# Edge convolution with features on partitions, its product turned on TensorE between the block sums

## What is computed

```python
h = x @ W_in                                                  # (N, 128)
W_ij = ssp(f_ij[:, 0, :] @ Wf1 + bf1) @ Wf2 + bf2             # (E, 128), f_ij has 32 values per edge
W_ij = W_ij * f_ij_cutoff                                     # one number per edge
x_ij = h[idx_j] * W_ij                                        # idx_j = dst: h of the sorted ends
out  = jax.ops.segment_sum(x_ij, idx_i, num_segments=N)       # idx_i = src: unsorted ends
y    = ssp(out @ Wo1 + bo1) @ Wo2 + bo2
x    = layernorm(x + y)
```

## Time and profile before

| | kernel before |
|---|---|
| median of three runs | 6694.08 us |
| the profiled execution, by its own time | 6709.68 us |
| its span in the profile | 6707.8 us |
| TensorE busy, share of the span | 61% |
| VectorE busy | 50% |
| ScalarE busy | 20% |
| GpSimd busy | 70% |
| mean granted TensorE clock | 0.669 of full speed |

### The profile page before, as it was taken

How to read it: one execution, slowest core, us unless ns; L and a number is a source line. 1 busy time by engine, 2 the same in 40 slices (tenths; PEclk the granted TensorE clock), 3 DMA queues, 4 the chain that set the end, 5 groups by cost and what they waited for, 6 DMA issues and landing times.

```text
span 6707.8 us, 70541 instructions
## 1 busy us (share of the span) xinstructions
PE 4086.0 (61%) x19983; PEld 3205.5 (48%) x19983; DVE 3357.6 (50%) x7053; ACT 1309.4 (20%) x3301; POOL 4716.8 (70%) x4809
## 2 busy tenths in 40 slices
PE   6444444444445543434343455688888879999997
PEld 3333333333333333333333344455555557777796
DVE  7333333333334655555555566533333346777697
ACT  2000000000001100000000000265555545555404
POOL 2777777777775477777777777677777777777604
PEclk9555555555556755555555577787777779999999
DMA  7222222222223422212222233333333347777696
GB/s 276 52 52 53 52 52 52 52 53 52 52 52 108 153 51 51 51 51 51 51 51 51 67 88 88 90 115 106 109 109 107 109 141 220 222 222 222 206 315 199
DMA packets 406899, 714.46 MB, mean 107 GB/s; under 512 B 103872, under 2 KB 180707, under 8 KB 405797
## 3 DMA queue, kind: packets, MB, share of 16 engines
q1 hardware_dynamic: 255622, 387.89, 18.6%
q0 software_dynamic: 150912, 322.24, 17.0%
HBM read 509.82 MB, written 199.90 MB: 106 GB/s over the span
## 4 chain that ended last, share of the span: by engine, by line
POOL 59%; PE 20%; issue 18%; DVE 1%; DMA 1%; ACT 0%; POOLq 0%; SPq 0%; DVEq 0%; ACTq 0%
POOL edge_rows L520 23%; POOL sorted_rows L563 13%; POOL buf_a L520 12%; POOL buf_x L520 11%; PE banks L1507 8%; PE banks L1561 3%; PE banks L1385 3%; PE banks L1496 3%; PE banks L1525 2%; PE banks L1558 1%; PE banks L1387 1%; POOL edge_rows L576 1%; POOL onehot L576 0%; DMA buf_a<-sorted_rows 0%; DVE first_place L780 0%
## 5 line engine op out<-in xcount | busy, mean ns | idle before, releaser
L520 POOL DMA_INDIRECT edge_rows<-messages,idx_stage x1568 | 1528.2, 975 | 686.9 <-issue 477.2
L1411 PE MATMUL banks<-onehot,edge_rows 128*128 128x128 f32 x3136 | 792.5, 432 | 1180.3 <-DMA edge_rows<-messages,idx_stage 1158.8
L1411 PEld LDWEIGHTS banks<-onehot,edge_rows 128*128 128x128 f32 x3136 | 679.9, 320 | 1305.9 <-DMA edge_rows<-messages,idx_stage 1284.3
L563 POOL DMA_INDIRECT sorted_rows<-edge_rows,idx_stage x784 | 777.9, 992 | 273.1 <-issue 231.7
L520 POOL DMA_INDIRECT buf_a<-messages,idx_stage x784 | 777.6, 992 | 238.9 <-issue 238.9
L563 POOL DMA_INDIRECT sorted_rows<-buf_a,idx_stage x784 | 776.4, 990 | 239.1 <-issue 232.7
L520 POOL DMA_INDIRECT buf_x<-messages,idx_stage x784 | 749.8, 956 | 238.9 <-issue 238.9
L939 DVE TENSOR_TENSOR buf_a<-buf_a,banks 128x128 f32 x392 | 113.1, 289 | 1307.7 <-PE banks L1411 1266.8
L1411 PE MATMUL banks<-x_onehot,buf_x 128*128 128x128 f32 x1568 | 406.8, 441 | 585.1 <-DMA buf_x<-messages,idx_stage 585.1
L1411 PE MATMUL banks<-x_onehot,buf_a 128*128 128x128 f32 x1568 | 389.9, 427 | 577.9 <-DMA buf_a<-messages,idx_stage 577.9
L1411 PEld LDWEIGHTS banks<-x_onehot,buf_x 128*128 128x128 f32 x1568 | 349.1, 328 | 642.8 <-DMA buf_x<-messages,idx_stage 642.8
(11 more groups left out here) (164 smaller groups left out, 5561.1 us busy)
## 6 DMA issues: line engine op xcount, KB each, us to landing
buf_a<-sorted_rows SPq DMA_DIRECT2D x593, 288.0 KB, 3.9
messages<-work SPq DMA_DIRECT2D x196, 320.0 KB, 2.2
buf_a<-dst_rows SPq DMA_DIRECT2D x198, 256.0 KB
buf_a<-in_attr SPq DMA_DIRECT2D x198, 128.0 KB
buf_a<-h_in SPq DMA_DIRECT2D x396, 64.0 KB
edge_rows<-messages,idx_stage POOLq DMA_INDIRECT x1568, 2.6
buf_x<-messages,idx_stage POOLq DMA_INDIRECT x784, 2.5
buf_a<-messages,idx_stage POOLq DMA_INDIRECT x784, 2.6
```

Source lines behind the costliest of these rows:

```text
L520: nc.gpsimd.indirect_dma_start(gathered[p][h][:, t, :], None, source, bass.IndirectOffsetOnAxis(ap=idx_stage[:, h, t:t + 1], axis=0),).the ...
L563: nc.gpsimd.indirect_dma_start(sorted_rows, bass.IndirectOffsetOnAxis(ap=idx_stage[:, 2 * u + h, t:t + 1], axis=0), msg_halves[2 * u + h][ ...
L1411: last = nc.tensor.matmul(ps_sums[slot][j], rows_in_slot[:, j * GROUP_TILES + t, :], hot[:, j * GROUP_TILES + t, :], start=(t == 0), stop= ...
```

## The change

The convolution now keeps features on partitions up to the product, and turns the product.

- TensorE expands h with two matmuls of 512 columns (`h_win` as weights, `spread` as moving data), so that `ps_h[j]` holds features by edges. It computes `ps_w[j]` with two matmuls of 512 columns (`wf2` as weights). The two bias matmuls are gone: `bf2` is loaded as a column.
- ScalarE copies `ps_h[j]` to `h_edge` unscaled, two activations of 512 columns, ahead of the softplus of the next half.
- VectorE forms `h_edge = (ps_w + bf2) * h_edge` in place, two instructions of 512 columns, and signals `s_prod`.
- TensorE turns each of the 8 tiles of `h_edge` back into `ps_h` (`nc.tensor.transpose` with the identity) and signals `s_turned`. In stage B its four block sums stand ahead of the first turn group (two of them), between the two turn groups (one), and behind them (one). `filter_in` of the next half stands ahead of all of these.
- ScalarE, after the softplus of the next half, copies the turned tiles with the cutoff as scale straight into the message slot, 8 activations of 128 columns, and signals `s_msg`. The wait for the slot's last scatter now also stands on ScalarE.
- TensorE's expansion of half k now waits for `s_msg` of half k-1, since `ps_h` holds the turned product until ScalarE has read it.
- VectorE's four `step_onehot` of a half stand together at its start, before the product, where they were spread over this half and the last one.
- SyncE's window load waits for the later of two `s_hexp` signals. The rows beyond a window (a branch that the trace does not take) are added on TensorE instead of VectorE.

The diff, without its declarations, the branch beyond the window and the bias splitting:

```diff
-        beside_bank = [0, 3, 0, 4]
+        beside_bank = [0, 4, 3, 0]
...
+            sp.dma_start(bf2[:, :], dram["bf2"].rearrange("o d -> d o")).then_inc(s_const_in, 16)
...
-                        sp.wait_ge(s_hexp, k + 1)
+                        sp.wait_ge(s_hexp, k * 2 + 2)
...
-                    k = r * 2 + h
+                    k, slot = r * 2 + h, r % 2 * 2 + h
+                    for j in range(2):
+                        act.wait_ge(s_hexp, k * 2 + (j + 1))
+                        act.wait_ge(s_turned, k * 2 + (j + 1))
+                        nc.scalar.activation(h_edge[:, j, :], ps_h[j], ACT.Copy).then_inc(s_hcopy, 1)
                     softplus_half(k + 1)
-                    act.wait_ge(s_hexp, k + 1)
+                    act.wait_ge(s_cut, k + 4)
+                    if r >= 2:
+                        act.wait_ge(s_scat[slot], scattered(r // 2))
                     for j in range(2):
-                        act.wait_ge(s_msg, k * 2 + (j + 1))
-                        act.wait_ge(s_cut, k + 4)
+                        act.wait_ge(s_turned, k * 2 + (j + 1 + SLOT2))
                         for t in range(GROUP_TILES):
-                            tile, i = slice(t * D, (t + 1) * D), j * GROUP_TILES + t
-                            last = nc.scalar.activation(h_edge[:, j, tile], ps_h[j][:, tile], ACT.Copy,
+                            i = j * GROUP_TILES + t
+                            last = nc.scalar.activation(msg_halves[slot][:, i, 0:D], ps_h[j][:, t * D:(t + 1) * D], ACT.Copy,
                                                         scale=cut_stage[:, h, i:i + 1])
-                        last.then_inc(s_hcopy, 1)
+                        last.then_inc(s_msg, 1)
...
-            def convolution_step(r, u, uses, beyond, adding=False, last_turn=False):
+            def convolution_step(r, u, uses, beyond, adding=False):
                 for h in range(2):
                     k = r * 2 + h
                     messages = msg_halves[2 * u + h]
                     if adding:
                         turn = r - (FIRST_ITERS + 1)
                         columns = load_columns(turn * STEP_SLOTS + 4 * h)
-
-                    def onehot_ahead(i):
-                        q = 4 * h + i
-                        if adding and not (last_turn and q >= STEP_SLOTS):
-                            step_onehot(turn * STEP_SLOTS + q, q % STEP_SLOTS, turn * 16 + 16 * (q // STEP_SLOTS + 1))
+                        for i in range(4):
+                            step_onehot(turn * STEP_SLOTS + (4 * h + i), 4 * h + i, turn * 16 + 16)
 
                     def add_step(i):
                         if adding:
                             q = 4 * h + i
                             add_segment(turn * STEP_SLOTS + q, q, columns[i], beside_bank[i])
 
-                    def message_group(j):
-                        dve.wait_ge(s_hcopy, k * 2 + (j + 1 + SLOT2))
-                        tiles = "p (t n) -> p t n"
-                        nc.vector.tensor_tensor(messages[:, j * GROUP_TILES:(j + 1) * GROUP_TILES, 0:D],
-                                                ps_w[j].rearrange(tiles, t=GROUP_TILES),
-                                                h_edge[:, j, :].rearrange(tiles, t=GROUP_TILES), ALU.mult
-                                                ).then_inc(s_msg, 1)
-
-                    spread_half(r + h, 1 - h)
-                    onehot_ahead(2)
-                    onehot_ahead(3)
-                    dve.wait_ge(s_hcopy, k * 2 + ((2 + SLOT2) if beyond else SLOT2))
-                    stage_cutoff(r + h, 1 - h)
                     if beyond:
                         spread_beyond(r, h)
-                    dve.wait_ge(s_cut, k + 4)
-                    add_step(0)
-                    onehot_ahead(4)
-                    soft_half(k + 1, 1 - h)
-                    add_step(1)
+                    for j in range(2):
+
+                        dve.wait_ge(s_hcopy, k * 2 + (j + 1))
+                        dve.wait_ge(s_w, k * 2 + (j + 1))
+                        nc.vector.scalar_tensor_tensor(out=h_edge[:, j, :], in0=ps_w[j], scalar=bf2[:, 0:1],
+                                                       in1=h_edge[:, j, :], op0=ALU.add, op1=ALU.mult).then_inc(s_prod, 1)
+                    spread_half(r + h, 1 - h)
+                    dve.wait_ge(s_msg, k * 2 + SLOT2)
+                    stage_cutoff(r + h, 1 - h)
 
                     if uses is not None:
                         dve.wait_ge(s_scat[2 * u + h], scattered(uses))
                     stage_indices(2, k, 2 * u + h)
                     nc.vector.tensor_copy(messages[:, :, D],
                                           src_idx[:, ds(r * ITER_TILES + h * HALF_TILES, HALF_TILES)]).then_inc(s_tagged, 1)
-                    dve.wait_ge(s_w, k + 1)
-                    message_group(0)
-                    message_group(1)
+                    add_step(0)
+                    add_step(1)
+                    soft_half(k + 1, 1 - h)
                     add_step(2)
-                    onehot_ahead(5)
                     add_step(3)
...
-                step_onehot(0, 0, 16)
-                step_onehot(1, 1, 16)
...
-            for s in (s_yc, s_sd, s_rsd, s_rows, s_x1, s_hrow, s_soft, s_fsoft, s_msg, s_hcopy,
+            for s in (s_yc, s_sd, s_rsd, s_rows, s_x1, s_hrow, s_soft, s_fsoft, s_msg, s_prod, s_turned,
...
+
             def convolution_step(r, beyond, adding):
                 for h in range(2):
                     k = r * 2 + h
+                    if adding:
+                        first = (r - (FIRST_ITERS + 1)) * STEP_SLOTS + 4 * h
+                    for j in range(2):
+
+                        pe.wait_ge(s_win_in[h], r * 32 + 32)
+                        pe.wait_ge(s_spread, k * 2 + (j + 1))
+                        pe.wait_ge(s_msg, k * 2 + (j + 1))
...
+                        nc.tensor.matmul(ps_h[j], h_win[:, h, j, :], spread[:, h, j * WIDE:(j + 1) * WIDE],
+                                         start=not beyond, stop=True).then_inc(s_hexp, 1)
+                    for j in range(2):
+
+                        pe.wait_ge(s_soft, k * 2 + (j + 1 + SLOT2))
+                        pe.wait_ge(s_prod, k * 2 + (j + 1))
+                        if adding:
+
+                            pe.wait_ge(s_added, first + SLOT2)
+                        nc.tensor.matmul(ps_w[j], wf2[:, :], soft_halves[h][:, j, :], start=True, stop=True).then_inc(s_w, 1)
                     filter_in(k + 1, 1 - h, (r + h) * 16 + 16)
                     if adding:
-                        first = (r - (FIRST_ITERS + 1)) * STEP_SLOTS + 4 * h
-                        sum_segment(first, 4 * h, beside_bank[0], first + (SLOT2 - 1))
+                        sum_segment(first, 4 * h, beside_bank[0])
                     for j in range(2):
 
-                        pe.wait_ge(s_win_in[h], r * 32 + 32)
-                        pe.wait_ge(s_spread, k * 2 + (j + 1))
-                        pe.wait_ge(s_hcopy, k * 2 + (j + 1))
+                        pe.wait_ge(s_prod, k * 2 + (j + 1 + SLOT2))
+                        if adding:
+                            sum_segment(first + (1 + j), 4 * h + (1 + j), beside_bank[1 + j])
                         for t in range(GROUP_TILES):
                             tile = slice(t * P, (t + 1) * P)
-                            last = nc.tensor.matmul(ps_h[j][:, tile], spread[:, h, j * WIDE + t * P:j * WIDE + (t + 1) * P],
-                                                    h_win[:, h, j, :], start=True, stop=True)
-                    last.then_inc(s_hexp, 1)
+                            last = nc.tensor.transpose(ps_h[j][:, tile], h_edge[:, j, tile], ident[:, :])
+                        last.then_inc(s_turned, 1)
                     if adding:
-
-                        pe.wait_ge(s_msg, k * 2 + SLOT2)
-                        sum_segment(first + 1, 4 * h + 1, beside_bank[1])
...
-                    for j in range(2):
-
-                        pe.wait_ge(s_soft, k * 2 + (j + 1 + SLOT2))
-                        pe.wait_ge(s_msg, k * 2 + (j - 1 + SLOT2))
-                        if beyond:
-                            pe.wait_ge(s_xadd, (k * 2 + 2) * BLOCKS + 1)
-                        if adding:
-
-                            pe.wait_ge(s_added, first + (2 * j + SLOT2))
-                        nc.tensor.matmul(ps_w[j], ones_rows[:, :], bias_rows[:, 0, :].unsqueeze(1).broadcast_to([3, 4, D]),
-                                         start=True, stop=False)
-                        for t in range(GROUP_TILES):
-                            last = nc.tensor.matmul(ps_w[j][:, t * D:(t + 1) * D], soft_halves[h][:, j, t * P:(t + 1) * P],
-                                                    wf2[:, :], start=False, stop=(t == GROUP_TILES - 1))
-                    last.then_inc(s_w, 1)
-                    if adding:
-                        sum_segment(first + 2, 4 * h + 2, beside_bank[2], first + (1 + SLOT2))
```

(20 more changed lines are left out.)

49 lines of the change are left out of this document (19 added, 30 removed).

## The result

The changed kernel takes 6865.45 us (median of 4 runs, 6860.8 to 6870.2), the kernel before 6694.74 (4 runs of the same series): ratio 1.0256, 95% interval 1.0244 to 1.0269, 170.7 us slower. The forecast was 6920 with a range of 6700 to 7070.

The account below looks back on a forecast made before the run. GpSimd's scatter, 10.37 us a half, was taken to bound the kernel. Stage A's 218 us (late start included) plus stage B's 8 made 226 on 6709.68, 6936; less the profiled run's 15.6 us, 6920 us, range 6700 to 7070.

Parts of the forecast that it names:

- stage A: Convolution from first scatter to first load of sorted rows, 112 halves: period 10.365 to 12.28 us, 212.6 us more.
- The closed ring of stage A: Expansion waits for the previous half's messages, whose softplus waits for `filter_in` behind that expansion: 10.1 us at full clock.
- F: Start of `filter_in` in a stage A half; first expansion claimed at F + 6.1, next `filter_in` at F + 10.1.
- The price of the low clock: Stage A's four matmuls behind TensorE's idle time start with 4.87 us at low clock: 2.36 us more a half.
- The later first message, 5.8 us: Start of stage A: filter, turns and copies delay the first message by about 5.8 us.
- Stage B, +8 us: From load of sorted rows to last scatter: TensorE's half becomes 10.59 us, clock stays 1.00, 8 us more.
- rival 4: GpSimd's scatter rows get cheaper as VectorE's L1147 moves off them: 41 us saved, 6653 us; chance 0.04.
- Rival 1: Stage A's clock holds or its chain is shorter; period stays at GpSimd's 10.37 us, 6708 us; chance 0.12.
- Rival 2: Low clock lasts over all four matmuls in stage A: period 13.5 us, 7056 us; chance 0.12.
- Rival 3: A turn costs four float32 passes: Stage B costs 95 us instead of 8, 7008 us; chance 0.10.
- Rival 5: Clock falls in Stage B too, half the time low: 15.9 us a half, 7350 us; chance 0.03.

Follow-up runs that it names:

- second profile of before: The unchanged kernel before, run and profiled again in the third series as a control: 6693.92 us (10 runs), stage A 10.34 us a half.
- fill: Changed kernel plus three extra 512-column matmuls, result unused, behind the turns of each stage A half from half 8: 6683.67 us, ratio to before 0.9987.
- banks: Changed kernel with stage A's turned products put into `ps_w` instead of `ps_h`, so the expansion no longer waits for messages: 6669.85 us, ratio to before 0.9966.
- order: Changed kernel with the next half's `filter_in` ahead of stage A's two expansions instead of behind them: 6669.98 us, ratio to before 0.9966.

## Why the prediction was right

The forecast was 6920, the measured time is 6865. The terms missed in the same direction, so nothing cancelled: stage A by 28 us, stage B by 17, the first message by 9 (spans, against the second profile of before). What decided the direction and most of the size, the ring and its low clock, was right.

- **The closed ring of stage A.** Right in every link: GpSimd waits for ScalarE, VectorE no longer waits for a slot. The forecast put the expansion at F + 6.1, it is at F + 6.04; at the full clock the ring was to take 10.1 us, fill shows 9.81. The 0.3 us too much is the second expansion, which I let wait for the second group of copies; the rows show the two back to back.
- **The price of the low clock.** The step that carries the result. Forecast 2.36 us a half, measured (11.34 + 12.55) / 2 - 9.81 = 2.13. The low clock lasted 5.6 us in one half and 3.4 in the next from the start of the expansion, where I took one value, 4.87, from rows 8. That the halves alternate was not forecast, and why they do stays open; only their mean comes near the 4.87. Period 11.99 over the whole stage instead of 12.28, so A cost 184.5 us and not 212.6.
- **The later first message, 5.8 us.** Wrong: it is about 3 us earlier. GpSimd stands idle for 31.68 us ahead of its first scatter, 34.67 and 34.71 in the two profiles of before; fill and banks, whose start is that of the changed kernel, show 31.61 and 31.64. The first half's expansion starts right behind the first `filter_in`, 3.72 us after it (4289.62 to 4293.34). In before it starts 10.6 us after it (4300.51 to 4311.12), behind the second `filter_in`, which waited for the softplus of the first (L1496 starting at 4307.44, 3.15 us idle). I had priced the added steps of the first message and not walked the start of the loop.
- **Stage B, +8 us.** Wrong in sign, by a small sum: -9. TensorE's half is 9.99 us and not 10.59. The three pairs take 5.44 instead of 5.73, the four block sums 3.67 (from 5992.89 on) instead of 3.96, and the turns 0.88, as chosen. A block sum took 0.99 in before ahead of the bias matmul, and also ahead of the expansion (5810.52 to 5811.51); here it takes 0.89 ahead of a turn or the wide expansion. Why the 0.99 did not transfer stays open. My reading of B was off as well. I called it bound by GpSimd with TensorE 0.1 us behind, but TensorE's half there is 10.43 us each time, while GpSimd's rows need 8 x (0.985 + 0.304) = 10.31. GpSimd works off the filled slots and is first held up by the product at 6149 (second profile of before). With 9.99 us TensorE is under GpSimd's pace. Of the gain of 9 us, 3.1 are cheaper rows (rival 4's mechanism), 2.6 two rows that were scattered ahead of the load, and 2.5 less idle time of GpSimd between its rows; the last 0.7 is where the load falls between two rows.
- **Rival 1, the clock holds.** It didn't in the changed kernel; the fill kernel is this rival made true by extra work, 6684 against the 6708 named for it; the difference is a stage B of 860.0 instead of 878.0 us and a first message 12.6 us earlier than I gave it (4302.15 against 4308.99 + 5.8), less 3.9 us by which its stage A is longer than that of before.
- **Rival 2, all four pairs low.** Every second half comes near it, with 6.51 of its 7.42 us.
- **Rival 3, a turn of four passes.** False: 0.44 us. The Trainium skill, page "TensorE: Matmul & The Clock Gate", section "Terms", states that the transpose mode is four times faster for FP32. The traces here show a factor of two, 0.44 us a group against 0.89 as plain matmuls, and they decide. A group took as long as its four weight loads of 0.11 us, which was the row I had chosen.
- **Rival 4, a cheaper row.** The reason against it, that GpSimd scatters all the time so there is nowhere to move to, was wrong: the long row hangs on when a row starts, not on whether GpSimd is busy. It gives 14 us in A and some 3 in B.
- **Rival 5, the clock falls in B.** False: 1.00 in 5700:6300 with the turns in place. The rule of the Trainium skill (page "TensorE: Matmul & The Clock Gate", section "Part 4: PE-mode transpose"), that a transpose does not count as work that keeps the clock up, is not refuted by this, since the turns are only 0.88 of 9.99 us. The low clock in B that I drew from it did not come.

## What to carry to other kernels

When a buffer gets a second use in the same step, follow the ring that it closes: whoever refills it now waits for the last reader of the second use, and slots further down don't help. Price that ring at the clock it will really run at, since idle time inside the ring lowers TensorE's clock and the matmuls behind the wait pay for it (2.13 us of 11.95 here). The cure may be as small as moving one independent step ahead of the waiting ones, or using the bank that is free first: either turned +171 us into -22.

## What the runs showed of the hardware

More work on TensorE made the kernel faster: 2.74 us of useless matmuls a half took stage A from 11.99 to 10.38 us a half. GpSimd's scatter row is 0.97 us or about 1.17, and nearly all long ones start while VectorE's conversion from int16 runs (before: 46 long rows of 465; order: 5 of 471); of the rows that start there, 77 of 78 were long in before and 36 of 75 in fill. A turn group of four transposes takes 0.44 us, the same group as plain float32 matmuls 0.89. And one chip ran the kernel before 18% slower than the other and turned the order of the kernels round: there the changed kernel was 3% faster than the kernel before, here it is 2.6% slower.
